# Q and K of a head group loaded in three transfers a side, and one store of normed rows kept for batch 0 alone

## What is computed

```python
# x: (8, 1024, 256) float32; H = 16 heads of HD = 16
qkv = x @ qkv_w.T                        # then rotary on q and k
heads 0..5    softmax(q k / 4)           # causal, all groups
heads 6..9    tq = sqrt(1/curv + |q|^2), tk likewise
              arg = max(-curv * (q k - tq tk), 1 + 1e-7)
              softmax(1 / (1e-6 + sqrt(1/curv) * arccosh(arg)))
heads 10..15  softmax(4 * qn kn)         # qn, kn normalized
x = layernorm(x + y @ proj_w.T + proj_b)
x = layernorm(x + ffn(x))                # ffn touches the first 1024 tokens,
                                         # that is batch 0: 8 experts, top 2, gelu
                                         # for all others it adds its bias alone
```

## Time and profile before

| what | value |
|---|---|
| median of 3 runs | 1947.89 us (1945.44 to 1950.06) |
| the profiled execution, its own time | 1950.01 us |
| its span, first to last instruction | 1948.4 us |
| PE / ACT / DVE / POOL busy | 83% / 72% / 62% / 39% |
| chain that ended last | PE 33%, issue 14%, DVE 9%, ACT 9%, POOL 7%, DMA 5% |
| mean granted TensorE clock | 0.919 |
| DMA packets | 75777, 215.01 MB |

### The profile page before, as it was taken

The page is one execution under the profiler, slowest core; times in us unless marked ns, Lnnn a source line. Parts: engine busy times, 40 slices in busy tenths (PEclk is TensorE's granted clock), DMA queues, the critical chain, the costliest instruction groups (busy, mean ns, idle before and its releaser), DMA issues.

```text
span 1948.4 us, 38980 instructions
## 1 busy us (share of the span) xinstructions
PE 1608.7 (83%) x13082; PEld 905.8 (46%) x13082; DVE 1203.7 (62%) x3014; ACT 1393.3 (72%) x1460; POOL 756.2 (39%) x369
## 2 busy tenths in 40 slices
PE   7999937876987898789779977986897789779993
PEld 4655612333443344344334433442443344369992
DVE  6877836634766686577657665765785577532234
ACT  2655638896897889788878987897889788851220
POOL 3344333443433444353435434344433465430003
PEclk9999959988997999899889988998998899779997
DMA  4699850255034405510650254054206511358893
GB/s 156 214 242 282 233 154 12 76 87 89 13 50 84 110 2 89 122 34 2 110 122 13 35 96 114 2 73 112 59 2 110 125 34 51 103 195 279 292 338 100
DMA packets 75777, 215.01 MB, mean 110 GB/s; under 512 B 18064, under 2 KB 27664, under 8 KB 69744
## 3 DMA queue, kind: packets, MB, share of 16 engines
q1 hardware_dynamic: 66400, 179.16, 37.5%
q0 software_dynamic: 9200, 33.43, 5.6%
HBM read 143.95 MB, written 68.58 MB: 109 GB/s over the span
## 4 chain that ended last, share of the span: by engine, by line
PE 33%; issue 14%; DVE 9%; ACT 9%; POOL 7%; DMA 5%; SPq 2%; DVEq 0%; POOLq 0%; ACTq 0%
PE a_o L1214 6%; PE a_w L1259 4%; PE a_s L715 4%; PE a_s L727 4%; PE a_s L1199 4%; POOL a_Z L1487 3%; POOL a_R L1484 3%; DVE a_X L1728 2%; PE a_w L1227 2%; PE a_w L1303 2%; DMA K<-t_parts 2%; ACT a_PT L1396 2%; SPq L1120 2%; DMA x_mid<-a_X 2%; ACT a_Z L1414 2%
## 5 line engine op out<-in xcount | busy, mean ns | idle before, releaser
L1396 ACT ACTIVATE a_PT<-a_s 128x1024 f32<-128x1024 f32 (+3 forms) x576 | 460.0, 810 | 154.3 <-PE a_s L1202 94.1
L1487 POOL TENSOR_TENSOR a_Z<-a_Z,a_R 128x2182 f32<-128x2182 f32 x64 | 290.0, 4531 | 449.0 <-ACT a_R L1408 442.2
L1199 PE MATMUL a_s<-Q,K 96*128 96x512 bf16 (+7 forms) x1152 | 330.7, 352 | 103.7 <-ACT a_PT L1396 75.5
L1484 POOL TENSOR_TENSOR a_R<-a_Z 128x2182 f32<-128x2182 f32 x64 | 245.1, 3830 | 242.1 <-DVE a_Z L1600 206.8
L1608 DVE TENSOR_REDUCE a_mx<-a_w 128x1 f32<-128x512 f32 (+2 forms) x576 | 307.3, 550 | 44.0 <-PE a_w L1227 37.7
L1214 PE MATMUL a_o<-a_PT,a_V 128*32 128x512 f32 (+3 forms) x2304 | 271.0, 545 | 74.8 <-ACT a_PT L1396 47.5
L1600 DVE TENSOR_SCALAR_CACHE_REDUCE a_Z<-a_w 128x512 f32<-128x512 f32 (+7 forms) x384 | 202.8, 528 | 116.8 <-PE a_w L1242 69.6
L1259 PE MATMUL a_w<-a_ident,a_R 128*128 128x128 f32 (+1 forms) x1152 | 202.5, 301 | 37.3 <-DVE a_PTh L1654 22.6
L1654 DVE COPY a_PTh<-a_w 128x512 f32<-128x512 f32 (+1 forms) x256 | 158.2, 622 | 102.0 <-PE a_w L1259 100.0
L1227 PE MATMUL a_w<-K,Q 96*128 96x512 bf16 (+2 forms) x576 | 188.8, 334 | 26.4 <-DVE a_mx L1608 10.1
L1199 PEld LDWEIGHTS a_s<-Q,K 99*128 99x128 bf16 (+1 forms) x1152 | 111.4, 103 | 198.8 <-ACT a_PT L1396 105.7
(11 more groups left out here) (166 smaller groups left out, 2539.9 us busy)
## 6 DMA issues: line engine op xcount, KB each, us to landing
qk_parts<-p_parts SPq DMA_DIRECT2D x128, 192.0 KB, 3.4
Q<-in_w SPq DMA_DIRECT2D x46, 512.0 KB, 6.2
K<-in_w SPq DMA_DIRECT2D x46, 512.0 KB, 7.4
Q<-qk_parts SPq DMA_DIRECT2D x144, 128.0 KB, 5.4
K<-qk_parts SPq DMA_DIRECT2D x144, 128.0 KB, 8.1
v_rows<-p_vt SPq DMA_DIRECT2D x8, 2048.0 KB, 9.7
a_V<-v_rows SPq DMA_DIRECT2D x32, 512.0 KB, 9.8
p_xT<-in_xt SPq DMA_DIRECT2D x8, 1024.0 KB, 8.3
```

The costliest lines, as they stand in the source:

```text
L1199: m = pe.matmul(sB[x % 2][:, i, 0:w], Kb[0:r, h, P * j:P * j + P], Qb[0:r, h, t0:t0 + w], start=True, stop=not diag)
L1396: act.activation(PT[:, u % 2, 2 * k:2 * k + 2, 0:w], sB[x % 2][:, :, 0:w], ACT.Exp, scale=scale_of(GROUPS[g][2 * k])).then_inc(prob.sem, 1)
L1484: pool.tensor_tensor(r, z, z, ALU.mult).then_inc(z_sq.sem, 1)
L1487: pool.tensor_tensor(z, z, r, ALU.add).then_inc(z_sum.sem, 1)
```

## The change

The six single transfers of a side become three. `PAIRS` lists (copies, part): Q's blocks 0 to 2 all hold part 0, blocks 3 and 4 part 1, block 5 part 2; K's blocks hold parts 0, 1, 2, then 0, 1, then 0. The six products are the same ones in another order. Q's source repeats one part with a step of zero, K's source steps over parts; in both, the number of copies (3, 2 or 1) is the outermost dimension of the source. The roots' rows go the same way. `mid_out` is done for batch 0 alone, `add_bias` of the others waits for the norm instead of the store, and ten late items move five slots up (`add_bias` four). For batch 0's case to be told apart, turn 1 of POOL and DVE is written out ahead of their loops.

```diff
-QPART = (0, 0, 1, 0, 2, 1)
-KPART = (0, 1, 0, 2, 0, 1)
-NPAIR = len(QPART)
+PAIRS = ((3, 0), (2, 1), (1, 2))
+NPAIR = sum(n for n, _ in PAIRS)
...
-    for qk, buf, order in ((0, Qb, QPART), (1, Kb, KPART)):
-        for r, part in enumerate(order):
-            src = qk_parts[bass.ds(b, 1), qk, part, 2 * BR * block:2 * BR * (block + 1), :]
-            src = src.rearrange("o (d h) t -> d (o h) t", d=HD)
+    def copies(src, n, first, same):
+
+        if same:
+            return src[first:first + 1].to_broadcast([n, *src.shape[1:]])
+        return src[0:n]
+
+    for qk, buf in enumerate((Qb, Kb)):
+        r = 0
+        for n, part in PAIRS:
+            src = qk_parts[bass.ds(b, 1), qk, :, 2 * BR * block:2 * BR * (block + 1), :]
+            src = src.rearrange("o s (d h) t -> (o s) d h t", d=HD)
             for h0, h1 in runs:
                 i0 = BLOCKS[block].index(h0)
-                found.append((g, buf, r * HD, (r + 1) * HD, (h0, h1, src[:, i0:i0 + h1 - h0, :])))
-    if g == 3:
-        for i in range(NPAIR):
-            for buf, first, order in ((Qb, 0, QPART), (Kb, N_HYP, KPART)):
-                found.append((g, buf, KR + i, KR + i + 1,
-                              (HYP0, COS0, t_parts[bass.ds(b, 1), order[i], first:first + N_HYP, :])))
+                found.append((g, buf, r * HD, (r + n) * HD,
+                              (h0, h1, copies(src[:, :, i0:i0 + h1 - h0, :], n, part, qk == 0))))
+            if g == 3:
+                src = t_parts[bass.ds(b, 1), :, qk * N_HYP:(qk + 1) * N_HYP, :].rearrange("o s h t -> (o s) h t")
+                found.append((g, buf, KR + r, KR + r + n, (HYP0, COS0, copies(src, n, part, qk == 0))))
+            r += n
...
-                         (121, ("add_bias",)), (123, ("statistics", 1, 0, NT // 2)), (124, ("statistics", 1, NT // 2, NT)),
-                         (125, ("variance", 1)), (126, ("inverse_root", 1)), (129, ("newton", 1)),
-                         (131, ("normalize", 1, 0)), (132, ("normalize", 1, 1)), (133, ("rows_out",)), (141, ("rows_in",))):
+                         (117, ("add_bias",)), (118, ("statistics", 1, 0, NT // 2)), (119, ("statistics", 1, NT // 2, NT)),
+                         (120, ("variance", 1)), (121, ("inverse_root", 1)), (124, ("newton", 1)),
+                         (126, ("normalize", 1, 0)), (127, ("normalize", 1, 1)), (128, ("rows_out",)), (136, ("rows_in",))):
...
-                    rows_out(d, x_mid, 0, mid_sent)
+                    if is_routed(d):
+                        rows_out(d, x_mid, 0, mid_sent)
...
-            with nc.Fori(1, B - 1, engines=[pool.engine], hint_back_edge=True) as b:
+            turn(1)
+            with nc.Fori(2, B - 1, engines=[pool.engine], hint_back_edge=True) as b:
...
-                    dve.wait_ge(mid_sent.sem, mid_sent.at(d))
+                    if is_routed(d):
+                        dve.wait_ge(mid_sent.sem, mid_sent.at(d))
+                    else:
+                        dve.wait_ge(normed.sem, normed.at(d, 0))
...
-            with nc.Fori(1, B, engines=[dve.engine], hint_back_edge=True) as b:
+            turn(1)
+            with nc.Fori(2, B, engines=[dve.engine], hint_back_edge=True) as b:
```

More of the change, by code:

```diff
@@ L987, in attend, with is_routed @@
                 "rows_out", "shift")
+        def is_routed(d):
+            return isinstance(d, int) and d == 0
         def is_late(item):
@@ L1563, in _ @@
             pool.wait_ge(spread_out, 16 * NCOL)
-            pool.wait_ge(mid_sent.sem, mid_sent.at(B - 1))
+            pool.wait_ge(mid_sent.sem, mid_sent.at(0))
             pool.wait_ge(out_sent.sem, out_sent.at(B - 1))
```

## The result

The changed kernel takes 2140.2 us, median of four runs (2137.9 to 2142.7), where the kernel before takes 1948.4 (1945.4 to 1950.1, four runs). The ratio is 1.097, with a 95% interval of 1.093 to 1.101: slower, by 192 us. The profiled execution took 2142.7 us with a span of 2141.0.

What follows compares the result with a forecast made beforehand. No engine is busy throughout, so turn length was taken to bound the kernel. Six turns +79, turn 1 +1.5 and projection +16 made 97 us on 1950.0: 2047, less 2.1 for the median, 2045 us; range 1965 to 2190.

Steps and rivals of the forecast that it cites:

- Engines by the outermost size: Head loads: the outermost dimension sets the DMA engines used, so the new transfers get 3, 2 and 16.
- Rival (b): Head loads: only one side is held to few engines, only turn 1 gains; about 1936 us, chance 0.04.
- Rival (a): Head loads: all 16 engines work and PE's wait for group 3 vanishes; 1916 us, chance 0.11.
- Deadline: When PE needs group 3, counted from SP's first issue R: shrinks from R + 18.4 to R + 15.5.
- Landing: Group 3's last data at R + 28.7, 0.59 MB an engine at 24 GB/s; PE waits 13.2 us a turn.
- rival (d): Group 3's loads: a single engine is fast and the moved slots give more; 1948 us, no change, chance 0.03.
- upper end: Group 3's latest landing, R + 41.0, with X's load as well and all at 18.2 GB/s.
- Slots: End of a turn: six store waits go, DVE stalls for newton, ACT waits less; 1.8 us gained in turns 2 to 7.
- clock, restart and slots together: Each of six turns: 3.1 us added for clock and restart after PE's wait, 1.8 us taken off for the slots.
- Turn 1: First turn, keeping the store to x_mid: group 3 lands at R + 28.7 against R + 27.2, +1.5 us.
- Projection: Batch 0's head loads keep one engine busy until 285.5, so attention starts later: +16 us (0 to +71).
- Rival (c): Loads of groups 0 and 1 spill past group 3's start under 21.7 GB/s an engine; 2186 to 2246 us, chance 0.08.

Runs made afterwards that it cites:

- e3: Changed kernel with the parts stored in another order, so that the three transfers a side run on all 16 engines: 1928.2 us, ratio 0.987.
- e9: Changed kernel with K's transfers single again, Q's three repeated ones kept and issued first: 2107.0 us, one run.
- e10: Changed kernel with Q's transfers single again, K's three stepped ones kept and issued last: 2079.6 us, one run.
- e7: e3 with X's load at the late slot 143: 1917.2 us, ratio 0.983.
- e4: Changed kernel with X's load and the store to out cut to one of eight row blocks from batch 1 on: 2107.3 us, one run.
- e1: Kernel before with the new three-transfer loads alone, slots and stores as before: 2170.0 us, one run.
- e2: Kernel before with only the store to x_mid for batch 0 alone and the moved slots, single transfers kept: 2011.7 us, ratio 1.032.
- e5: e2 with X's load put back to a late slot, 143 instead of 136: 1971.7 us, ratio 1.010.
- e8: Changed kernel with batch 0's head loads, issued in the projection, as single transfers: 2084.6 us, one run.
- e12: e10 with the K side issued before the Q side, so that the few-engine transfers go first: 2093.9 us, one run.

## Why the prediction was right, and where it was off

The direction, the cause and the count of engines were right, and 2140.2 us lies within 1965 to 2190. The size was not: the forecast of 2045 us has about half of the slowdown, 97 of 192 us.

**Engines by the outermost size.** Right: 3, 2 and 16, by the packet counts, and e3 shows that this is the cause. Where the prediction chose 3 between 3 and 16, the row with an outermost size of 3 was the one to go by. Rival (b), one side only, fell with e9 and e10. Rival (a) gave 1916 us for spread loads; the run that is the changed kernel with them is e3, 1928.2. That e7 has 1917.2 is a match with another kernel, in which X's load is moved as well. The 130 GB/s that (a) read for 16 partitions are those of several transfers at once, to six blocks of 16 partitions a side, and say little of one such transfer.

**Deadline.** R + 15.5 forecast, R + 15.5 in turn 3.

**Landing, the term that was mis-sized.** Forecast R + 28.7, measured R + 38.0. The 0.59 MB of an engine: 30.7 us with X's load and the store to out light (e4), instead of 24.6, 6.1 us. The two at full size: 5.9 us where 2.7 stood for the store to out, 3.2 more. 6.1 + 3.2 is the 9.3 us that were missing, and the wait is 22.5 us instead of 13.2. The reasoning "an engine whose neighbours are idle should be above the mean" is right as it stands: 24.6 to 26.2 GB/s in such stretches (880:886, 908:914, 938:946), close to the 24 taken and to rival (d)'s 26.6. What was wrong is the assumption that they are idle through the landing. At its start, with group 3's own spread parts under way, an engine moves 15.1 GB/s (886:894 of e4), beside X's load 12.9 (900:906 of the changed kernel), and 918:924 has 19.4. X's load stood in the upper end alone. It would have lain within the landing at either slot: e1, with X's load at R + 18, lands at R + 37.3. Turn 1's R + 27.2 with X's load at R + 4.3 was the row that showed what it costs beside such loads.

**Slots.** The movements were foreseen: DVE stands for POOL's newton before the second norm, and ACT's wait for `square` goes. DVE and POOL at the end of turn 2:

```profile
886.73 1.38 DVE L1741 TENSOR_SCALAR a_X<-a_X,a_mv,a_rs 128x256 f32<-128x256 f32 x4 [4.41 <-POOL a_rs L1516]
```

```profile
880.73 4.85 POOL L1498 TENSOR_TENSOR a_Z<-a_Z,a_R 128x2182 f32<-128x2182 f32 x1 [12.88 <-ACT a_R L1419]
...
898.49 0.93 POOL L1482 DMA_DIRECT2D a_X<-in_x  x1
```

PE's idle time ahead of the last value product, 6.34 us in turn 1 and 5.99 in turn 7, is 2.73 in both. But "1.8 gained a turn" failed as a gain of this kernel: e2 and e5 show that what is saved ahead of a load that hangs on R is only waited, and with single transfers the moved X load costs some 37 us. Forecast for the clock, restart and slots together +1.3 a turn; measured about 0.1.

**Turn 1.** Forecast +1.5, measured +12.2. X's load lay beside group 3 already; the landing goes from R + 27.2 to R + 34.6 all the same, and the wait is 6.9 us longer (17.62 and not 10.73). The rest is mostly DVE's wait for the one store to x_mid that is kept, 10.6 us and not some 3.4, a cost on another queue that was not in the sum.

**Projection.** Forecast +16 (0 to +71), measured +54. SP's last stores of parts:

```profile
315.48 5.19 SPq L162 DMA_DIRECT2D qk_parts<-p_parts  x8
```

They were at 261.36. The prediction asked when the busiest engine would be through. It named in one clause that a transfer of x queued behind waits, and gave that no price; it is what happened. The loads of heads delay the transfers of x behind them, PE waits (44.9 us in four, the longest 23.8), and the next parts come later still. e8, in which only these loads are single again, is 56 us faster, and its wait for x is 0.2 us.

**Rival (c), the spill.** SP is held for long while it issues groups 0 and 1 (start, length):

```profile
842.40 20.55 SPq L1131 DMA_DIRECT2D Q<-qk_parts  x6
...
863.13 11.15 SPq L1131 DMA_DIRECT2D K<-qk_parts  x6
```

The rival wanted a pace under 21.7 GB/s. From SP's first issue of group 0 in this turn, 836.50, the loads were through at about 891: 1.15 MB in some 53 us, 21.8 GB/s, and R is 894.06. So it missed by little. The mean of 19.2 in e4 is that of group 3, with more beside it, and is not the pace here. There was also a little more room than the 52.9 us of the row: 57.6 here, 57.9 on the mean of the six turns where it was 53.8. The turns are 21 us longer, but most of that lies behind R and gave groups 0 and 1 no time. In turn 1 the room was 47.6 us (R = 485.40), and there the spill did come: 485:490 has 100 packets, 76 - 20 = 56 of them of the 4 KB that group 1 and V have and group 3 has not:

```profile
DMA packets 100, 0.43 MB, mean 87 GB/s; under 512 B 20, under 2 KB 20, under 8 KB 76
```

The sum: 52 instead of 16 for the projection (the end of turn 0), 128 instead of 79 for six turns, 12.2 instead of 1.5 for turn 1. The 16 of the projection, the 79 of the six turns and the 1.5 of turn 1 were all too small, and for one reason: each transfer on few engines was costed on its own engine, and not for what queues behind it or lies beside it.

## What to carry to other kernels

Before joining small transfers into one with an added outer dimension of 2 or 3, look at how many engines it will use; where the copies can be laid out in DRAM so that they merge with the next dimension (48, 32), the joined transfer is a small gain (here 0.7% by itself, 1.3% to 1.8% with the rest of the change), and where they can't it is a loss far larger than the issue time saved (here 9.7% with the rest of the change). When a step is moved in the order of an engine, ask of each DMA that it issues which critical load it will then lie beside (of the 58 us that e2 lost, 37 went with a late X). In the profile, a low DMA share with an engine waiting on a DMA is the sign; the count of small packets names the transfer.

## What the hardware showed beyond that

- What slows an engine is the traffic beside it. With two engines busy each moved 25.4 GB/s (880:886, packets of 4 KB) and 26.2 (938:946, packets of 8 KB), against 20.8 with all busy; beside X's load it was 12.9 (900:906). The number of busy engines alone doesn't decide: with three busy it was 19.4 in 918:924 of the changed kernel and 25.7 in 909:915 of e4. What makes that difference was not tried.
- A transfer on few engines delays those on all engines beside or behind it: the 1 MB store to x_mid, which another queue issues, from 5.1 to 9.8 us (e1), and PE's wait for x from 4.1 to 44.9 us.
- It also holds the engine that issues: the six DMAs of group 1's Q side took SP 20.55 us, where before its twelve took 7.29 (the row is from turn 3 of the kernel before):

```profile
935.45 7.29 SPq L1120 DMA_DIRECT2D Q<-qk_parts  x12
```

- With the same transfers, the few-engine side issued last lands 2 to 5 us earlier than issued first (e9 to e12, one turn of each).
